# The entry of layer two in a one-core two-layer kernel: where unit 0's first projections are written, when its gate weights are made, and which engine adds four of its pieces

## What is computed

```
x = x + tanh(g_xattn[1]) * L1_xattn(layernorm(x), ctx, ctx, mask, ...)
x = x + tanh(g_ffn[1])   * L1_ffn(layernorm(x), sim_matrix, gates, q_proj, k_proj, v_proj, o_proj)

def L1_ffn(hidden, ...):            # n tokens, 16 experts e
    logits = norm(hidden) @ norm(sim_matrix) - sigmoid(gates)
    w = softmax(where(mask > 0, relu(logits), -inf))      # gate weights, n x 16
    q, k, v = [sum_e w[:, e] * (hidden @ p[e]) for p in (q_proj, k_proj, v_proj)]
    o = softmax(q @ k.T / sqrt(128)) @ v                  # within a sequence
    return sum_e (w[:, e] * o) @ o_proj[e]
```

## Time and profile before

| | |
|---|---|
| median of 3 runs | 1690.09 us (1688.3 to 1690.72) |
| the profiled execution | 1690.68 us, span 1689.0 us |
| busy share of the span | PE 94%, PEld 82%, DVE 72%, ACT 64%, POOL 70% |
| layer two's loop | from about 588 us to the end |
| mean granted clock of TensorE | 0.976 |

### The profile page before, as it was taken

One profiled execution on the slowest core, in us unless ns is written; L12 is line 12 of the kernel. 1 busy time (PEld: TensorE's weight loads), 2 busy tenths in 40 slices (PEclk: granted clock), 3 DMA queues, 4 the chain that ended last, 5 costly groups with the idle time before them and its releaser, 6 DMA issues.

```text
span 1689.0 us, 50848 instructions
## 1 busy us (share of the span) xinstructions
PE 1590.5 (94%) x15944; PEld 1388.4 (82%) x15945; DVE 1208.1 (72%) x3915; ACT 1079.9 (64%) x2725; POOL 1179.0 (70%) x1715
## 2 busy tenths in 40 slices
PE   6999999986998689999999999999999999999996
PEld 4777777765998479888888898889888889888885
DVE  3677777753555357887888888888788888877785
ACT  3777777753555456666666666666666666766654
POOL 3555555532455567888888888888788878887785
PEclk9999999986999899999999999999999999999998
DMA  2322222234553100000000000000000000000000
GB/s 74 108 70 71 70 69 75 75 108 113 145 140 84 30 14 17 14 17 17 20 15 17 17 18 17 17 17 14 20 14 17 17 20 14 17 17 11 5 8 10
DMA packets 92101, 68.95 MB, mean 41 GB/s; under 512 B 13936, under 2 KB 87696, under 8 KB 91920
## 3 DMA queue, kind: packets, MB, share of 16 engines
q1 hardware_dynamic: 76512, 49.34, 10.0%
q0 software_dynamic: 5120, 12.62, 2.4%
q10 hardware_dynamic: 10288, 4.74, 1.0%
HBM read 35.74 MB, written 22.52 MB: 34 GB/s over the span
## 4 chain that ended last, share of the span: by engine, by line
PE 84%; DVE 6%; issue 4%; POOL 2%; ACT 1%; DMA 1%; SPq 1%; DVEq 0%; POOLq 0%; ACTq 0%
PE s_bank L1858 13%; PE s_bank L1859 12%; PE s_bank L1860 12%; PE po L1682 8%; PE tb L1667 6%; PE s_bank L1800 4%; PE po L1812 4%; PE s_bank L1647 4%; PE s_bank L1998 2%; PE m L1621 1%; PE m L1708 1%; PE s_bank L1989 1%; PE tb L1858 1%; PE m L1606 1%; PE s_bank L1656 1%
## 5 line engine op out<-in xcount | busy, mean ns | idle before, releaser
L727 POOL TENSOR_TENSOR qkv<-qkv,scaled 128x384 f32<-128x384 f32 x480 | 490.3, 1021 | 134.1 <-ACT scaled L1001 97.6
L1001 ACT ACTIVATE scaled<-s_bank,wg 128x384 f32<-128x384 f32 x448 | 256.6, 582 | 128.6 <-PE s_bank L1860 127.1
L1858 PE MATMUL s_bank<-proj_hi,hn_hi 128*128 128x384 f32 x896 | 329.8, 368 | 1.2 <-DVE qkv L1440 0.9
L1440 DVE SCALAR_TENSOR_TENSOR qkv<-s_bank,wg,qkv 128x384 f32<-128x384 f32 x448 | 273.6, 611 | 49.0 <-PE s_bank L1860 37.6
L1859 PE MATMUL s_bank<-proj_lo,hn_hi 128*128 128x384 f32 x896 | 302.4, 337 | 0.0
L1860 PE MATMUL s_bank<-proj_hi,hn_lo 128*128 128x384 f32 x896 | 300.9, 336 | 0.0
L862 ACT ACTIVATE pT<-tb 128x512 f32<-128x512 f32 x256 | 152.1, 594 | 164.7 <-PE tb L1667 97.2
L1858 PEld LDWEIGHTS s_bank<-proj_hi,hn_hi 128*128 128x128 f32 x896 | 168.6, 188 | 15.8 <-ACT scaled L1001 5.9
L1859 PEld LDWEIGHTS s_bank<-proj_lo,hn_hi 128*128 128x128 f32 x896 | 169.3, 189 | 3.0
L1860 PEld LDWEIGHTS s_bank<-proj_hi,hn_lo 128*128 128x128 f32 x896 | 168.3, 188 | 0.0
L1667 PE MATMUL tb<-ident,prob 128*128 128x128 f32 x1024 | 157.6, 277 | 5.2 <-ACT pT L862 5.0
(11 more groups left out here) (284 smaller groups left out, 3819.8 us busy)
## 6 DMA issues: line engine op xcount, KB each, us to landing
xs<-sorted_in SPq DMA_DIRECT2D x71, 128.5 KB, 2.1
kx<-kT SPq DMA_DIRECT2D x256, 32.0 KB
sorted_out<-yo SPq DMA_DIRECT2D x71, 64.0 KB, 1.6
xin<-in_x SPq DMA_DIRECT2D x32, 128.0 KB
cin<-in_ctx SPq DMA_DIRECT2D x32, 128.0 KB, 2.3
ctx_cols<-xcT SPq DMA_DIRECT2D x32, 128.0 KB
w<-in_L_ffn_W SPq DMA_DIRECT2D x16, 256.0 KB, 3.9
xcT<-ctx_cols SPq DMA_DIRECT2D x32, 128.0 KB, 2.3
```

Of the source, the lines that this page charges most:

```text
L727: g.tensor_tensor(into, into, scaled[m % SCALED][:, 0:cols], ALU.add).then_inc(dense_added, 1)
L1001: ins = act.activation(into, bank[:, 0:3 * D], ACT.Copy, scale=wg[v % 4][:, 1, k:k + 1])
L1440: v.scalar_tensor_tensor(out=acc, in0=bank[:, 0:3 * D], scalar=wg[w % 4][:, 0, k:k + 1], in1=acc, op0=ALU.mult, op1=ALU.add).then_inc(dens ...
L1858: pe.matmul(bank[:, 0:cols], hi[:, tile], of(proj_hi), start=True, stop=False)
```

## The change

It touches unit 0 of layer two only; units 1 to 31 keep their order, banks and engines.

1. Unit 0's pieces 0 and 1 of both tiles go to the four score banks instead of `tb` and `po`, and PE does them ahead of the loop, behind `upper_values(2)` and in front of `upper_heads(1)`. They wait for unit 1's last exponential (`exp_ready` 8). `upper_scores(0)` now waits until two pieces of each tile have been taken out.
2. On VectorE, `normalise` of unit 1 stands behind `gate_shift`, and `gate_softmax(0)` comes before `add_residual(1)`, which moves into `body1(0)` with `second_stats(1)`, behind three pieces.
3. For tile 1 of unit 0, pieces 1 to 4 are taken, weighted and added by VectorE in one instruction each (`take_second`), which also counts `dense_added`; ScalarE's four copies to `scaled` and GpSimd's four additions of those pieces go.
4. On ScalarE, piece 0 of tile 1 comes ahead of `copy_xT(3)` and `apply_second_norm(1)`.

In the diff's order: the two helpers; GpSimd's `add_part`; ScalarE's `take_part`, `body1` and the end of its work ahead of the loop; VectorE's new `take_second` and its `body1`; PE's `part`, `upper_scores`, `body1` and the work ahead of its loop.

```
+        def bank_of(u, t, kind, k):
+            if kind == "q" and k < 2 and u > 0:
+                return entry_bank[t]
             return part_bank[t][k % 2]
+        def vector_adds(u, kind, k):
+            return u == 0 and kind == "q" and 1 <= k < 5
...
             def add_part(u, kind, k):
-                if exists(u if kind == "q" else u - 1):
+                if exists(u if kind == "q" else u - 1) and not vector_adds(u, kind, k):
...
-                if exists(v):
+                if exists(v) and not vector_adds(u, kind, k):
                     if kind == "q" and k == 0:
                         act.wait_ge(f["w_ready"], u + 1)
+                    if vector_adds(u, kind, k - 1):
+                        act.wait_ge(dense_used[1], part_no(u, kind, k))
...
             def body1(u):
                 take(u, "q", 0)
+                if u == 0:
+                    copy_xT(3)
+                    apply_second_norm(1, 1, lambda t: x3[1][:, t, :], lambda t: hn[:, t, :])
                 exp_bank(u + 2, 0)
...
             apply_norm(1, 3, 1)
-            copy_xT(3)
-            apply_second_norm(1, 1, lambda t: x3[1][:, t, :], lambda t: hn[:, t, :])
             upper_units(act, body1)
...
+            def take_second(u, *ks):
+                for k in ks:
+                    if vector_adds(u, "q", k):
+                        n = part_no(u, "q", k)
+                        v.wait_ge(dense_filled[1], n + 1)
+                        v.wait_ge(dense_used[1], n)
+                        acc = qkv[u % 2][1][:, :, :].rearrange("p c n -> p (c n)")
+                        v.scalar_tensor_tensor(out=acc, in0=bank_of(u, 1, "q", k)[:, 0:3 * D],
+                                               scalar=wg[u % 4][:, 1, k:k + 1], in1=acc, op0=ALU.mult, op1=ALU.add)\
+                            .then_inc(dense_used[1], 1)
+                        v.wait_ge(dense_used[1], n + 1)
+                        v.sem_inc(dense_added, 1)
...
                 take(u, "q", 0)
+                if u == 0:
+                    take(u, "q", 1)
+                    take_second(u, 1)
+                    add_residual(1, 1, 1, x3[1][:, :, :])
+                    second_stats(1, 1, x3[1])
                 max_bank(u + 2, 1)
...
-                take(u, "q", 1, 2, 3, 4)
+                if u != 0:
+                    take(u, "q", 1)
+                take(u, "q", 2, 3, 4)
+                take_second(u, 2)
                 if exists(u + 1):
                     gate_norm(u + 1, gates)
                 take(u, "q", 5)
+                take_second(u, 3)
                 if exists(u + 1):
                     gate_logits(u + 1, gates)
                 if exists(u + 1):
                     gate_top(u + 1, gates)
                 total_groups(u - 2)
+                take_second(u, 4)
                 take(u, "q", 6)
...
-                    if kind == "q" and k == 0:
+                    if kind == "q" and k < 2 and u == 0:
+                        pe.wait_ge(s[1]["exp_ready"], 8)
+                    elif kind == "q" and k == 0:
...
-                        wait(pe, dense_used[t], parts_until(u))
+                        wait(pe, dense_used[t], 2 if u == 0 else parts_until(u))
...
                 token_transposes(u - 1)
-                tokens_parts(u, 0, 0)
-                tokens_parts(u, 1, 0)
+                if u != 0:
+                    tokens_parts(u, 0, 0)
+                    tokens_parts(u, 1, 0)
                 upper_scores(u)
...
             upper_values(2)
+            tokens_parts(0, 0, 0)
+            tokens_parts(0, 1, 0)
+            tokens_parts(0, 0, 1)
+            tokens_parts(0, 1, 1)
             upper_heads(1)
```

More of the change, by code:

```diff
@@ L342, in added_no @@
             return before + (k - 1 if kind == "q" else (E1 - 1) * exists(u) + k - 1)
-        def bank_of(t, kind, k):
-            if kind == "q":
-                return entry_bank[t] if k < 2 else part_bank[t][k % 2]
+        def bank_of(u, t, kind, k):
+            if kind == "q" and k < 2 and u > 0:
+                return entry_bank[t]
             return part_bank[t][k % 2]
+        def vector_adds(u, kind, k):
+            return u == 0 and kind == "q" and 1 <= k < 5
         def slots(eng, body, load=None, split=None, late=0):
@@ L997, in take_part @@
                         wait(act, dense_added, added_no(u, kind, k) - SCALED + 1)
-                    bank, part = bank_of(1, kind, k), scaled[added_no(u, kind, k) % SCALED]
+                    bank, part = bank_of(u, 1, kind, k), scaled[added_no(u, kind, k) % SCALED]
                     if kind == "q":
@@ L1428, in take_part @@
                 if exists(w):
-                    n, bank = part_no(u, kind, k), bank_of(0, kind, k)
+                    n, bank = part_no(u, kind, k), bank_of(u, 0, kind, k)
                     v.wait_ge(dense_filled[0], n + 1)
@@ L1539, in _ @@
             gate_top(0, gates)
-            normalise(s[1], 1)
             gate_index(gates)
             gate_shift(gates)
+            normalise(s[1], 1)
             gate_mask(gates)
-            add_residual(1, 1, 1, x3[1][:, :, :])
             gate_softmax(0, gates, wg[0])
-            second_stats(1, 1, x3[1])
             upper_units(v, body1)
@@ L1850, in part @@
                         pe.wait_ge(dense_used[t], part_no(u, kind, k - 2) + 1)
-                    tile, bank = slice(P * t, P * t + P), bank_of(t, kind, k)
+                    tile, bank = slice(P * t, P * t + P), bank_of(u, t, kind, k)
                     if kind == "q":
@@ L2017, in body1 @@
                 token_transposes(u - 1)
-                tokens_parts(u, 0, 0)
-                tokens_parts(u, 1, 0)
+                if u != 0:
+                    tokens_parts(u, 0, 0)
+                    tokens_parts(u, 1, 0)
                 upper_scores(u)
-                tokens_parts(u, 0, 1)
+                if u != 0:
+                    tokens_parts(u, 0, 1)
                 upper_normed(u + 1)
-                tokens_parts(u, 1, 1)
+                if u != 0:
+                    tokens_parts(u, 1, 1)
                 subtract_bank(u + 2, 1)
```

## The result

| | before | the change |
|---|---|---|
| median of 14 runs each | 1690.14 us (1685.53 to 1693.94) | 1692.64 us (1691.35 to 1696.07) |
| ratio to before | | 1.0015, 95% interval 1.0008 to 1.0022 |
| profiled execution, span | 1690.68 us, 1689.0 us | 1692.72 us, 1691.0 us |

The time lies in the predicted range, 0.7 us under its upper end, and within 0.2% of before. The sign was right, and the size three times the forecast: +2.5 us where the sum said +0.85.

What follows compares the result with a forecast made beforehand. TensorE's unbroken run in unit 0, followed by GpSimd's 16.0 us chain, was taken as the bound. An earlier run start (-0.66 us) and a low clock (+1.5 us) gave +0.85 us, so 1690.9 us, range 1687.0 to 1693.3.

Steps and rivals of the forecast that it cites:

- The sign: Whole kernel: the forecast said slower, by about +0.85 us.
- the sum: Unit 0 of layer two: -0.66 us for the run's start and +1.5 us for the clock, giving +0.85 us.
- The bound: Unit 0: TensorE's unbroken run, then GpSimd's 16.0 us chain from piece 5 to `token_transposes(0)`.
- The rival that it would come through: GpSimd in unit 0: four additions removed shorten its chain by 4.0 us, giving 1685.4 us; chance 0.06.
- Four pieces in the old hole: TensorE ahead of `upper_heads(1)`: four pieces, 2.1 us, fill its 2.14 us wait and make nothing behind late.
- TensorE thus begins to subtract at 593.57 instead of 594.23: -0.66 us: Start of TensorE's unbroken run in unit 0: first maxima subtracted 0.66 us earlier, in effect one piece less before it.
- four hand-overs, each 0.15 us dearer: Semaphore hand-overs ahead of the run: if four cost 0.15 us more each, the run's shift could be 0.
- The clock, "+1.5 us": TensorE's unbroken run in unit 0: new holes drop the clock to 1.2 GHz, costing 1.5 us, bounds 0 and +2.6.
- The rival that it stays high: TensorE's clock at unit 0's entry: no fall behind the new holes, giving 1689.4 us; chance 0.33.
- VectorE's pieces 2 to 4, hidden: VectorE in unit 0: three added pieces of 0.61 us fit its 2.6 us wait for TensorE, costing 0.
- The rival of VectorE as the limit: Unit 0: VectorE's four pieces, 2.4 us, land on TensorE's run and prolong the low clock, giving 1694.4 us; chance 0.06.
- Unit 1 opens at the low clock as before: TensorE at the start of unit 1: low clock after its wait for GpSimd, as before, with no added time.

Runs made afterwards that it cites:

- e2: The kernel before, entry unchanged, with VectorE adding pieces 1 to 4 of unit 0's second tile: 1794.26 us, ratio 1.0011 to the kernel before.
- e6: The kernel before, own entry, with VectorE adding pieces 5 to 7 of unit 0's second tile: 1792.89 us, ratio 0.9980 to the kernel before.
- e4: The kernel before with twelve unused products filling TensorE's 2.1 us hole ahead of `upper_heads(1)`: 1791.42 us, ratio 1.0002 to the kernel before.
- e8: The changed kernel with unused products filling all TensorE's holes at the entry (3, 5 and 13): 1796.26 us, ratio 1.0008 to the kernel before.
- e1: The changed kernel with only piece 1 added by VectorE, pieces 2 to 4 back on ScalarE and GpSimd: 1795.07 us, ratio 1.0017 to the kernel before.
- e3: The changed kernel with twelve unused products on TensorE in the hole behind unit 2's scores only: 1793.32 us, ratio 1.0009 to the kernel before.
- b1: The kernel before, code unchanged, run and profiled once more: 1690.26 us, ratio 1.0001.
- a1: The changed kernel, code unchanged, run and profiled once more: 1692.04 us, ratio 1.0007 to the kernel before.
- e9: The changed kernel with unit 1's residual and statistics ahead of VectorE's three pieces, and TensorE's entry holes filled: 1691.03 us, ratio 1.0006 to the kernel before.

## Why the prediction was right, and which term was not

**The bound: right.** TensorE's unbroken run, then GpSimd's chain. From the first addition to `token_transposes(0)` the change takes 622.36 - 606.38 = 15.98 us and e2 16.0, where 16.0 was forecast; TensorE still waits 3.62 us. GpSimd's freed time became 9.55 us of idling ahead of that addition. Its start, 607.66 in times of before (1.28 us added to those of the change), is 0.9 us behind the forecast's 606.8, by the two steps that follow. The rival that it would come through is false, by e2, and e6 shows what would have made it true.

**Four pieces in the old hole: right.** They fill it (582.95 to about 585.2), with nothing late behind.

**"TensorE thus begins to subtract at 593.57 instead of 594.23: -0.66 us": this step failed.** Measured: 11.36 against 11.44, -0.08 us. In times of before the residual began at 589.60, not 589.25, and `upper_normed(1)` ran at 593.82, not 593.35. I had ScalarE's piece 0 as the last of the hand-overs, and the pieces of tile 0 as fitting before it. But in the change's own times ScalarE ended at 587.18 and VectorE began its tile 1 piece only at 587.49: VectorE's own chain was last. In it each of the steps that depend on each other costs more than its duration: 0.11 us from the softmax's last step to the first piece, 0.11 to the second, and 0.23 us from the tile 1 piece to the residual, which waits until that piece is written so that it can be counted. Residual to `hn` took 4.08 us (4.04 forecast) and the hand-over to TensorE another 0.14. The prediction named this itself as the way to 0: four hand-overs, each 0.15 us dearer. The Trainium skill, "VectorE: DVE Perf Modes", on the TRN2 errata, would make the three pieces shorter, by an estimate from its formula 0.525 us each; the trace has 0.61 to 0.62 and does not agree, and by the page the step would have been missed by more.

Behind that lies a wrong reading of before. The piece of 0.63 us that stood between `upper_normed(1)` and the subtraction did go: from the one to the other it is 0.17 us now (592.54 to 592.71) and was 0.85 (593.22 to 594.07). But I let the new `hn` cancel against the moment at which TensorE ran `upper_normed(1)` before, 593.38, and `hn` had been there earlier, at 592.04 + 0.88 = 592.92:

```profile
592.04 0.88 ACT L854 ACTIVATE hn<-x,shiftb,rstdb 128x128 f32<-128x128 f32 x2 [2.76 <-POOL shiftb L605]
```

TensorE, at the low clock, was 0.3 us late for it (0.14 us of the 0.46 is the hand-over). Since `gate_products(0)`, `hn` is complete at +10.29 us before and at +11.05 in the change, 0.76 us later, and that eats up the piece. e4 shows the same from the other side: given the high clock, TensorE stood 1.01 us for `hn`. At equal clock the order is worth nothing (e8 39.42, e4 39.25).

**The clock, "+1.5 us": right.** It fell behind the two new holes, 0.8 us after TensorE had begun again, was at 1.2 GHz from about 593.4 to 596.8, and cost 1.6 us (the change against e8). The rival that it stays high has not occurred in the change's two profiles; e8 gives its price, and it would have been no gain but 0.0 (39.42 against 39.31 and 39.43 of before). That the clock falls just there is in part luck: the same code ahead of it gave another moment in e1 and e3. "TensorE: Matmul & The Clock Gate", Part 1, of the Trainium skill says of such a ramp that it is under 1% of a typical kernel's span, and not to fit to a specific count of slow matmuls. It is 0.1% here, as the page says; and it was nearly all there was to forecast.

**VectorE's pieces 2 to 4, hidden: right.** The logits were written at 601.34 + 0.38 = 601.72 us, and `upper_values(3)` ran at 602.80: a margin of 1.1 us where 1.2 was forecast. e1 against e8 (27.97 and 28.07 us) agrees. The rival of VectorE as the limit is false.

**"Unit 1 opens at the low clock as before": half right, and the second missing term.** It opens low, but for longer, which makes 36.3 to 36.4 us to the next unit against 35.5 to 35.8: +0.7 us that the sum didn't have. The table under b1 and a1 shows that the low clock accounts for it. In b1, the kernel before, the stretch at 1.2 GHz is as long as in the change, 6.8 us; but there the clock falls 2.9 us ahead of `token_transposes(0)`, inside TensorE's wait, in the change only 1.8 us and in a1 1.4 us ahead of it. Whether the new entry makes it fall late, or chance does, is open: two profiles of each kernel can't tell, and e9, with the change's pieces and a high clock in unit 0, took 35.80 us.

The sum by what was measured: -0.1 + 1.6 + 0.7 = +2.2 us at `token_transposes(1)` (77.34 against 75.02 us in the mean of two profiles each, +2.3), with +2.5 us in the first medians and +1.35 in the repeated ones. So the forecast was right on what bounds unit 0 and on its largest term, the clock. The other two terms, the run's start and unit 1, were 0.6 and 0.7 us too low, and the range was wide enough to hold both.

## What to carry to other kernels

Before you count a shortened queue as a gain, find what the place waits for once the engine there is fast: a low clock can make an engine look like the bound where a chain through three others ends only 0.3 us sooner. A hole is not free where it is moved to; one in front of a wait hides the low clock that it brings, and the same hole in front of an unbroken run pays for it in full. When work is taken off a late engine, take it from behind its last idle moment, since what stands ahead of that only makes the engine idle longer.

## What the runs showed of the hardware

- Filling holes on TensorE with products that nobody reads keeps the clock up and is cheap: e8's 21 fillers of about 0.19 us turned granted 0.50 into 1.00 and won 1.6 us up to `token_transposes(0)`, and delayed nothing where they were done before the operand came. In e3, 12 of them came behind a hole that was left open, too late, and took 2.98 us where e4's 12 took 2.36.
- The clock also falls when a burst stands between two holes: 0.97 us idle, 1.7 us of scores, 2.64 us idle, and the fall 0.8 us later. The moment differs between executions of like code (+12.0 and +12.2 us in the change's two profiles, +7.3 us in e3), and so does what the fall costs.
- The same program takes 1690 us on one chip and 1792 to 1795 on others, 6% more, with a mean granted clock of 0.95 to 0.96 against 0.977. Unit 0's 39.3 us are the same on all. The later units aren't: 34.04 us on the one, 35.7 on the others, at a granted clock of 1.00 on both. In e4 TensorE waits 1.15 us in such a unit for VectorE's first maximum; in the kernel before on the first chip it has no wait there. What VectorE waits for in e4 the profile doesn't name. Layer one differs too: `gate_products(0)` comes at 641.00 us in e4 and at 582.63 before.
